# Layer 0's attention: row scores on 128 rows and two per column tile, output transposes two heads later

## The chip, the core and the metric

The kernel runs on one core of one Trainium2 chip. The metric is the device time of one execution in microseconds, as the median of several runs. Inside the core five engines work side by side and wait for each other through semaphores: TensorE (PE, matmuls and transposes into PSUM), VectorE (DVE), ScalarE (ACT), GpSimd (POOL) and SyncE (SP, which issues the DMAs). A matmul on TensorE has a weight load of its own (PEld), which may run beside an earlier matmul.

## What is computed

The whole kernel is two layers of attention and feed-forward work on x of 2 x 1024 x 128. The change touches the attention of layer 0 alone: 16 heads of width 8, causal, on 2 batches.

```python
def _L0_attn_ref(x, Wq, bq, Wk, bk, Wv, bv, Wo, bo):      # batch 2, seq 1024, 16 heads of 8
    q = x @ Wq.T + bq
    k = x @ Wk.T + bk
    v = x @ Wv.T + bv
    q, k, v = (split(q), split(k), split(v))
    scores = jnp.einsum('bhqd,bhkd->bhqk', q, k) / jnp.sqrt(jnp.float32(HEAD_DIM))
    scores = jnp.where(mask, scores, jnp.float32(NEG))     # causal
    attn = jax.nn.softmax(scores, axis=-1)
    out = jnp.einsum('bhqk,bhkd->bhqd', attn, v)
    out = out.transpose(0, 2, 1, 3).reshape(batch, seq, D_MODEL)
    return out @ Wo.T + bo

x = x + _L0_attn_ref(xn, ...) + _L0_ffn_ref(xn, ...)
```

## The kernel before

The program is a row of stages, each with its own block: projections of layer 0, attention of layer 0 (`attend_layer0`), experts, projections of layer 1, trees, attention of layer 1, and the end. Attention of layer 0 goes over 32 heads (2 batches x 16), one head after the other. Each engine has its own program, written out by hand as a `section(n, ...)` for each head n; four sections stand ahead of a loop, the loop holds four (`heads`), and five stand behind it (the last, n = 32, only finishes). Nothing but the order of the code and the semaphores sets what runs when.

Each score is computed twice. First the **row scores** (`row_unit`, L350, with the causal mask added by a second matmul, L353): the queries lie on partitions, 12 units of 128 to 512 keys per head, into two PSUM banks `ps_row` that are used in turn. VectorE reads each unit for its maximum (`peaks`, L463), so a unit can be written only when the unit two before it has been read (`row_read`). From the maxima VectorE makes a shift in three bfloat16 parts (L466 to L472, `shift_ready`). TensorE turns the shift into a row (L394, eight small matmuls of 3 weight columns), and ScalarE copies it into three spare rows of q, partitions 64 to 66 (L439); k holds ones there. So the second computation, the **column scores** (L407 and mask L410, 128 rows of contraction, keys on partitions, 8 tiles of 1024 down to 128 queries, two PSUM buffers `ps_col` in turn), comes out with the row maximum taken off. ScalarE takes the exponent of each tile (L445). The row scores use partitions 0 to 63 of q and k only, so the shift rows of an older head in the same q slot don't disturb them. q and k have four slots; SyncE loads the q and k of a head four ahead.

The **value products** of head n-1 (`pv`, L374, 32 output columns each, three groups) stand behind column tiles 0, 2 and 4 of head n. ScalarE copies their result from PSUM (L451, `oT`) between the exponents of tiles 5 and 6. TensorE turns `oT` by eight transposes of float32 (L424) into the same two `ps_row` banks, and VectorE adds up the four parts, divides and stores (`keep`, L481 to L487).

In section n of TensorE the order is: turn of head n's shift, two row units of head n+1, then each column tile of head n followed by one row unit of head n+1 (two behind tiles 0 and 2) and by a value product where one is due, then the transposes of head n-1 at the end. VectorE reads the 12 units of head n+1, makes its shift, then keeps head n-1. `row_base` counts the uses of `ps_row` for all of them.

## Time and profile before

| | |
|---|---|
| time, median of 3 runs | 2847.52 us (2844.19 to 2849.03) |
| profiled execution, its own time | 2842.8 us |
| its span, first to last instruction | 2840.7 us |
| attention of layer 0, first row unit to last store | 80.9 to 535.9 us |
| a steady head, query copy to query copy | 13.53 us |
| busy in 300 to 350 us: TensorE, VectorE, ScalarE, GpSimd | 46.30, 29.75, 25.14, 0.76 us |
| granted TensorE clock from 300 to 350 us | 1.00 of full |

The page cuts the span into 40 slices. Layer 0's attention lies in slices 2 to 8; TensorE is busy nine tenths or more in most of them, and PEclk is the share of full clock that it was granted:

```profile
PE   6799999999889688837676667667666766676668
...
DVE  4555655311245567668878787878887787878870
ACT  2345445433224133255656465656555564656543
...
PEclk7699999999879789966565666666665656665658
```

### The profile page before, as it was taken

To read this page: it belongs to the slowest core of one execution; us is meant where nothing else is said; L and a number is where in the kernel's file an instruction comes from. 1 tells how busy PE (TensorE), PEld (TensorE's weight loads), DVE (VectorE), ACT (ScalarE), POOL (GpSimd) and SP (SyncE) were. 2 spreads that over 40 slices of the span, in tenths; PEclk is the share of its full clock that TensorE was granted. 3 is DMA by queue.
4 is the path that set the end of the run, shared out by engine and by line. 5 is a ranking of instruction groups with operands and counts; after the bars stand their busy time and mean duration, and the time that the engine had idled before them with its cause. 6 is when DMAs were issued, how large, how long until landed. Compare 5 with 4: busy or idle time off the path is not lost. (4 is left out here: it accounts for less than half of the span.)

```text
span 2840.7 us, 38498 instructions
## 1 busy us (share of the span) xinstructions
PE 2149.0 (76%) x10704; PEld 1409.8 (50%) x10704; DVE 1863.7 (66%) x4939; ACT 1351.1 (48%) x2755; POOL 912.2 (32%) x708
## 2 busy tenths in 40 slices
PE   6799999999889688837676667667666766676668
PEld 3233333477654355515555454545554554555458
DVE  4555655311245567668878787878887787878870
ACT  2345445433224133255656465656555564656543
POOL 0000000000014100026455555556554645455650
PEclk7699999999879789966565666666665656665658
DMA  5000000100002000000000000000000000000000
GB/s 169 20 15 14 17 14 11 31 1 0 37 30 86 34 0 0 9 22 16 9 15 8 16 8 13 11 8 15 8 15 8 15 8 15 8 16 8 1 1 23
DMA packets 34022, 53.59 MB, mean 19 GB/s; under 512 B 9269, under 2 KB 15287, under 8 KB 33848
## 3 DMA queue, kind: packets, MB, share of 16 engines
q1 hardware_dynamic: 33847, 51.90, 6.3%
q14 instruction: 142, 1.16, 0.1%
q8 instruction: 33, 0.54, 0.1%
HBM read 34.04 MB, written 17.83 MB: 18 GB/s over the span
## 5 line engine op out<-in xcount | busy, mean ns | idle before, releaser
L1313 ACT ACTIVATE a_trash<-a_sc,a_search 128x1024 bf16<-128x1024 f32 (+6 forms) x672 | 548.5, 818 | 494.6 <-DVE a_npeak L1563 338.1
L1202 PE MATMUL a_ps_o<-g_v,a_kT 128*128 (+1 forms) x2304 | 501.6, 378 | 240.1 <-ACT a_kT L1330 235.1
L1202 PEld LDWEIGHTS a_ps_o<-g_v,a_kT 128*128 128x128 f32 x2304 | 458.0, 289 | 316.4 <-ACT a_kT L1330 262.4
L1191 PE MATMUL a_ps_t<-g_ident,a_prob 128*128 128x128 f32 x1152 | 286.2, 389 | 164.5 <-DVE a_prob L1547 164.5
L1179 PE MATMUL a_ps_s<-a_k,a_q 128*128 128x512 f32 (+3 forms) x768 | 359.9, 598 | 46.3 <-DVE a_sc L1557 34.1
L1261 POOL TENSOR_SCALAR a_work<-a_sc,a_thr 128x640 f32<-128x640 f32 (+3 forms) x128 | 213.1, 1669 | 505.8 <-POOLq L1291 505.8
L1244 POOL TENSOR_SCALAR a_prob<-a_sc,a_found 128x768 f32<-128x768 f32 (+4 forms) x160 | 282.9, 1768 | 223.1 <-POOLq L1242 223.1
L463 DVE TENSOR_REDUCE a_top<-a_ps_row 128x1 f32<-128x512 f32 (+3 forms) x384 | 207.5, 558 | 161.1 <-PE a_ps_row L353 107.2
L1191 PEld LDWEIGHTS a_ps_t<-g_ident,a_prob 128*128 128x128 f32 x1152 | 225.1, 230 | 174.5 <-issue 150.2
L1557 DVE TENSOR_SCALAR_CACHE_REDUCE a_sc<-a_ps_s 128x1024 f32<-128x1024 f32 (+7 forms) x256 | 193.3, 755 | 132.8 <-PE a_ps_s L1181 126.1
L1330 ACT ACTIVATE a_kT<-a_ps_t 128x512 f32<-128x512 f32 (+3 forms) x384 | 179.7, 476 | 204.7 <-PE a_ps_t L1191 204.6
L1179 PEld LDWEIGHTS a_ps_s<-a_k,a_q 128*128 128x128 f32 x768 | 151.5, 227 | 192.3 <-issue 114.6
L445 ACT ACTIVATE a_prob<-a_ps_col 128x1024 f32<-128x1024 f32 (+7 forms) x256 | 158.3, 653 | 148.5 <-PE a_ps_col L407 115.7
L1251 POOL TENSOR_TENSOR a_prob<-a_sc,a_prob 128x768 f32<-128x768 f32 (+4 forms) x160 | 201.9, 1270 | 0.0
L1323 ACT ACTIVATE a_prob<-a_sc,a_npeak 128x1024 f32<-128x1024 f32 (+7 forms) x256 | 180.6, 771 | 5.2 <-DVE a_sorted L1475 5.2
L938 POOL TENSOR_TENSOR p_full<-p_ra,p_rb 128x512 f32<-128x512 f32 x40 | 50.5, 1264 | 374.8 <-DVE p_rb L888 371.6
L331 POOL COPY a_v<-l_v 128x72 f32 (+1 forms) x32 | 8.0, 251 | 506.8 <-PE a_ps_out L374 428.7
L1547 DVE SCALAR_TENSOR_TENSOR a_prob<-a_sc,a_thr,a_prob 128x1024 f32<-128x1024 f32 (+2 forms) x96 | 124.5, 1326 | 65.2 <-issue 65.1
L1268 POOL TENSOR_TENSOR a_prob<-a_prob,a_work 128x640 f32<-128x640 f32 (+3 forms) x128 | 151.3, 1192 | 0.0
L584 ACT ACTIVATE ex_hid<-ex_ps_h,le_b 128x512 f32<-128x512 f32 x128 | 87.5, 687 | 128.1 <-PE ex_ps_h L561 127.8
L350 PE MATMUL a_ps_row<-a_k,a_q 64*128 64x512 bf16 (+3 forms) x384 | 132.4, 346 | 13.5 <-DMA a_k<-stack 12.5
L635 DVE SCALAR_TENSOR_TENSOR l_acc<-ex_ps_y,l_comb,l_acc 128x128 f32 x112 | 31.9, 345 | 151.4 <-PE ex_ps_y L552 151.1
(247 smaller groups left out, 3780.6 us busy)
## 6 DMA issues: line engine op xcount, KB each, us to landing
q1turned<-p_full SPq DMA_DIRECT2D x32, 256.0 KB, 2.0
a_q<-q1turned SPq DMA_DIRECT2D x32, 256.0 KB, 3.6
a_k<-k1turned SPq DMA_DIRECT2D x32, 256.0 KB, 4.0
stack<-p_parts SPq DMA_DIRECT2D x24, 256.0 KB, 3.8
a_q<-stack SPq DMA_DIRECT2D x32, 96.0 KB, 2.1
a_k<-stack SPq DMA_DIRECT2D x32, 96.0 KB, 2.2
le_w<-d_w SPq DMA_DIRECT2D x1, 2048.0 KB, 8.7
k1turned<-p_full SPq DMA_DIRECT2D x8, 256.0 KB, 2.0
```

The lines of the kernel that those rows point to most:

```text
L445: act.activation(prob[:, p, PO[j]:PO[j] + S - j * P], ps_col[:, (p + j + 1) % 2, 0:S - j * P], ACT.Exp, scale=SCALE).then_inc(col_read, 1)
L463: m = dve.tensor_reduce(top[:, i, c:c + 1], ps_row[:, u % 2, 0:width], AX.X, ALU.max)
L1179: pe.matmul(ps_s[:, j % 2, c:c + w], q[:, p, i * P:width], k[:, p, c:c + w], start=True, stop=True)
L1191: m = pe.transpose(ps_t[:, x % 2, a * P:(a + 1) * P], columns(prob, p, i)[:, (c + a) * P:(c + a + 1) * P], g.ident[:, :])
L1202: m = pe.matmul(outs[i // 4][:, i % 4, :], kT[:, x % 2, a * P:(a + 1) * P], v[:, bass.ds((n // GRP) * (TB * VW1) + (c + a) * VW1, VW1)], s ...
L1244: pool.tensor_scalar(columns(prob, p, i), columns(sc, p, i), found[:, i - 1:i], None, ALU.is_gt).then_inc(marked, 1)
L1251: pool.tensor_tensor(columns(prob, p, i), columns(sc, p, i), columns(prob, p, i), ALU.subtract).then_inc(aside, 1)
L1261: pool.tensor_scalar(marks(j), columns(sc, p, i), thr[:, i - 1:i], None, ALU.is_ge).then_inc(cut_marked, 1)
L1313: act.activation(trash[:, (p * NTAL + u) % 2, 0:(i + 1) * P], columns(sc, p, i), ACT.Sign, scale=-1.0, bias=trials[:, p, c, i - 1:i], accu ...
L1323: act.activation(columns(prob, p, i), columns(sc, p, i), ACT.Exp, scale=1.0 / DOWN, bias=npeak[:, p, i:i + 1]).then_inc(p_ready, 1)
L1330: act.activation(kT[:, x % 2, 0:cnt * P], ps_t[:, x % 2, 0:cnt * P], ACT.Copy).then_inc(t_read, 1)
L1557: dve.tensor_scalar(columns(sc, p1, i), ps_s[:, j % 2, 0:(i + 1) * P], SCALE, None, ALU.mult, ALU.max, accum_out=peak[:, p1, i:i + 1]).the ...
```

## The change

- Row units use all 128 rows of q and k. For that, the three shift rows of a q slot have to be zero again before the next head's row units: a zero tile `none` is added, and GpSimd writes zeros (`none + none`) into partitions 64 to 66 of the slot once all column tiles of its head are done (`clear`, semaphore `cleared`); the first row unit of a head waits for it.
- Behind every column tile stand two row units, until the 12 are used up (behind tile 4); behind tiles 5, 6 and 7 stand none.
- The transposes and the keeping of a head stand two sections later, and inside: TensorE turns head n-2 in section n behind column tile 0 and row units 2 and 3, ahead of the value product (`turn`); VectorE keeps it between its readings of units 3 and 4. Units 4 to 11 count two uses of `ps_row` later. In sections 0 and 1 there is none; section 32 has two.

```diff
+        none = r.sb("none", [P, S], BF16)
...
+        FIRST = 4
...
         def row_base(n):
-            if is_at(n, 0):
-                return NU
+            if is_at(n, 0) or is_at(n, 1):
+                return (n + 1) * NU
             if is_at(n, NH):
                 return row_base(NH - 1) + 2
-            return n * (NU + 2) + (NU - 2)
+            return n * (NU + 2) + (NU - 4)
+
+        def turn_base(n):
+            rows = not (is_at(n, NH - 1) or is_at(n, NH))
+            return row_base(n) + (FIRST if rows else 0)
...
+                def clear(n, h):
+                    pool.wait_ge(v_ready, n + 2)
+                    pool.wait_ge(col_ready, n * CU + CU)
+                    pool.tensor_tensor(q[SHIFT0:SHIFT0 + NSH, h, :], none[SHIFT0:SHIFT0 + NSH, :],
+                                       none[SHIFT0:SHIFT0 + NSH, :], ALU.add).then_inc(cleared, 1)
+                    pool.wait_ge(cleared, n + 1)
...
+                    for h in range(NQ):
+                        clear(i * NQ + (h - 2), (h + 2) % NQ)
+                        values(i * NQ + h, h % 2)
...
                     if u == 0:
                         pe.wait_ge(qk_in[h], i4 * 32 + 32)
+                        wait(pe, cleared, i4 * NQ + (h - NQ + 1))
                     wait(pe, row_read, unit - 1)
-                    last = pe.matmul(ps_row[:, u % 2, 0:width], q[0:SHIFT0, h, i * P:(i + 1) * P],
-                                     k[0:SHIFT0, h, c * CH:c * CH + width], start=True, stop=True)
+                    last = pe.matmul(ps_row[:, u % 2, 0:width], q[:, h, i * P:(i + 1) * P],
+                                     k[:, h, c * CH:c * CH + width], start=True, stop=True)
...
+                def turn(n, base):
+                    pe.wait_ge(out_read, n + 1)
+                    for x in range(2):
+                        pe.wait_ge(row_read, base + (x - 1))
+                        for i in range(4):
+                            m = pe.transpose(ps_row[:, x, i * P:(i + 1) * P],
+                                             oT[:, (4 * x + i) * P:(4 * x + i + 1) * P], g.ident[:, :])
+                        m.then_inc(row_ready, 1)
...
-                        rows_ahead(2 if j in (0, 2) else 1)
+                        rows_ahead(2)
+                        if j == 0 and not (is_at(n, 0) or is_at(n, 1)):
+                            turn(n - 2, turn_base(n))
                         if j in (0, 2, 4) and not is_at(n, 0):
                             pv(n - 1, 1 - p, j // 2)
                     rows_ahead(NU)
-                    if not is_at(n, 0):
...
+                    if is_at(n, NH):
+                        turn(NH - 1, turn_base(NH) + 2)
...
-                                act.wait_ge(row_ready, row_base(n - 1) + (2 if is_at(n, NH) else NU + 2))
+                                act.wait_ge(row_ready, turn_base(n) + 2)
...
                     for u, (i, c) in enumerate(UNITS):
+                        if u == FIRST and between is not None:
+                            keep(between, base + FIRST)
+                            base = base + 2
...
+                    turned = None if is_at(n, 0) or is_at(n, 1) else n - 2
                     if rows:
-                        peaks(n + 1, 1 - h % 2, row_base(n))
-                    if not is_at(n, 0):
-                        keep(n - 1, row_base(n) + (NU if rows else 0))
+                        peaks(n + 1, 1 - h % 2, row_base(n), turned)
+                    else:
+                        keep(turned, turn_base(n))
+                    if is_at(n, NH):
+                        keep(NH - 1, turn_base(n) + 2)
```

Three places show what the change makes of the instruction streams. A row is the line, the operation, its output and inputs and the output's size (`x4`: four in a row; REGISTER_ALU and ISA rows prepare or test a count). In the changed kernel the row unit is L372 with mask L375, the transposes L408, the value product L396, the column tile L440 with mask L443, and the shift's turn L427.

TensorE behind column tile 0, before:

```order
L350 MATMUL a_ps_row<-a_k,a_q 128x384
L353 MATMUL a_ps_row<-g_maskq,g_identb 128x128
L69 REGISTER_ALU
L350 MATMUL a_ps_row<-a_k,a_q 128x512
L353 MATMUL a_ps_row<-g_maskq,g_identb 128x128
L374 MATMUL a_ps_out<-a_prob,a_v 32x512 x4
L407 MATMUL a_ps_col<-a_q,a_k 128x512
```

The same place in the changed kernel:

```order
L372 MATMUL a_ps_row<-a_k,a_q 128x384
L375 MATMUL a_ps_row<-g_maskq,g_identb 128x128
L69 REGISTER_ALU
L372 MATMUL a_ps_row<-a_k,a_q 128x512
L375 MATMUL a_ps_row<-g_maskq,g_identb 128x128
L406 REGISTER_ALU
L408 MATMUL a_ps_row<-g_ident,a_oT 128x128 x4
L406 REGISTER_ALU
L408 MATMUL a_ps_row<-g_ident,a_oT 128x128 x4
L396 MATMUL a_ps_out<-a_prob,a_v 32x512 x4
L440 MATMUL a_ps_col<-a_q,a_k 128x512
```

The eight transposes now stand between row unit 3 and the first value product.

TensorE at the end of a head, from column tile 7 to the turn of the next head's shift, before:

```order
L407 MATMUL a_ps_col<-a_q,a_k 128x128
L410 MATMUL a_ps_col<-g_maskk,g_identb 128x128
L69 REGISTER_ALU
L350 MATMUL a_ps_row<-a_k,a_q 128x512
L353 MATMUL a_ps_row<-g_maskq,g_identb 128x128
L422 REGISTER_ALU
L424 MATMUL a_ps_row<-g_ident,a_oT 128x128 x4
L422 REGISTER_ALU
L424 MATMUL a_ps_row<-g_ident,a_oT 128x128 x4
L69 ISA
L392 REGISTER_ALU
L394 MATMUL a_ps_col<-g_identb,a_shift 3x128 x8
```

And in the changed kernel, from column tile 5 on:

```order
L440 MATMUL a_ps_col<-a_q,a_k 128x384
L443 MATMUL a_ps_col<-g_maskk,g_identb 128x128
L69 REGISTER_ALU
L440 MATMUL a_ps_col<-a_q,a_k 128x256
L443 MATMUL a_ps_col<-g_maskk,g_identb 128x128
L69 REGISTER_ALU
L440 MATMUL a_ps_col<-a_q,a_k 128x128
L443 MATMUL a_ps_col<-g_maskk,g_identb 128x128
L69 ISA
L425 REGISTER_ALU
L427 MATMUL a_ps_col<-g_identb,a_shift 3x128 x8
```

The last three column tiles stand in a row, with no row unit and no transpose between them and the shift's turn.

VectorE, from the end of a head's shift to the next unit, before (L472 makes the last part of the shift, L481 to L487 keep a head):

```order
L472 TENSOR_TENSOR a_shift<-a_left,a_shift 128x8
L69 REGISTER_ALU
L479 REGISTER_ALU
L481 TENSOR_REDUCE a_osum<-a_ps_row 128x36
L479 REGISTER_ALU
L481 TENSOR_REDUCE a_osum<-a_ps_row 128x36
L484 RECIPROCAL a_rec<-a_osum 128x8
L487 ISA
L487 REGISTER_ALU
L487 TENSOR_TENSOR l_o<-a_osum,a_rec 128x8x8
L462 ISA
L463 TENSOR_REDUCE a_top<-a_ps_row 128x1
```

In the changed kernel the keeping (L511 to L517) stands between the readings of units 3 and 4 (L493):

```order
L493 TENSOR_REDUCE a_top<-a_ps_row 128x1
L509 REGISTER_ALU
L511 TENSOR_REDUCE a_osum<-a_ps_row 128x36
L509 REGISTER_ALU
L511 TENSOR_REDUCE a_osum<-a_ps_row 128x36
L514 RECIPROCAL a_rec<-a_osum 128x8
L517 ISA
L517 REGISTER_ALU
L517 TENSOR_TENSOR l_o<-a_osum,a_rec 128x8x8
L492 REGISTER_ALU
L493 TENSOR_REDUCE a_top<-a_ps_row 128x1
```

The keeping moved from behind the shift to the middle of the next head's readings.

## Rows read from the trace of the kernel before

**Rows 1.** Windows: start:end, length, busy us (instructions) by engine, PEclk, DMA.

```profile
81.00:114.60 33.60, 28.61 (x102) 9.15 (x101) 17.32 (x39) 10.45 (x13) 0.00 (x0) 0.50 0.09 16
...
300.00:350.00 50.00, 46.30 (x313) 18.11 (x313) 29.75 (x77) 25.14 (x36) 0.76 (x3) 1.00 0.04 12
380.90:384.30 3.40, 2.52 (x19) 1.29 (x18) 1.92 (x10) 1.45 (x2) 0.00 (x0) 1.00 0.05 17
384.30:387.70 3.40, 3.40 (x14) 0.60 (x13) 1.24 (x2) 0.58 (x1) 0.00 (x0) 0.50 0.00 0
```

**Rows 2.** Timeline of TensorE, one head. Start, us, engine, line, out<-in, count, idle before.

```profile
315.50 0.39 PE L407 MATMUL a_ps_col<-a_q,a_k 128*128 128x512 bf16 x1 [0.41 <-ACT a_q L439]
315.72 0.22 PE L410 MATMUL a_ps_col<-g_maskk,g_identb 128*128 128x128 bf16 x1
315.78 0.38 PE L407 MATMUL a_ps_col<-a_q,a_k 128*128 128x512 bf16 x1
316.09 0.33 PE L350 MATMUL a_ps_row<-a_k,a_q 64*128 64x384 bf16 x1
316.36 0.23 PE L353 MATMUL a_ps_row<-g_maskq,g_identb 128*128 128x128 bf16 x1
...
316.99 1.07 PE L374 MATMUL a_ps_out<-a_prob,a_v 128*32 128x512 f32 x8
317.99 0.39 PE L407 MATMUL a_ps_col<-a_q,a_k 128*128 128x512 bf16 x1
...
321.01 0.39 PE L407 MATMUL a_ps_col<-a_q,a_k 128*128 128x512 bf16 x1
...
323.38 0.34 PE L407 MATMUL a_ps_col<-a_q,a_k 128*128 128x384 bf16 x1
...
325.47 1.37 PE L424 MATMUL a_ps_row<-g_ident,a_oT 128*128 128x128 f32 x8
327.32 0.61 PE L394 MATMUL a_ps_col<-g_identb,a_shift 128*3 128x128 bf16 x8 [0.47 <-DVE a_shift L472]
```

**Rows 3.** Timeline of VectorE, the same head's last readings and its shift.

```profile
324.24 1.89 DVE L463 TENSOR_REDUCE a_top<-a_ps_row 128x1 f32<-128x384 f32 x3 [1.03 <-PE a_ps_row L353]
...
327.09 0.17 DVE L472 TENSOR_TENSOR a_shift<-a_left,a_shift 128x8 bf16<-128x8 f32 x1
```

**Rows 4.** Timeline of ScalarE, the same head.

```profile
314.43 1.01 ACT L439 ACTIVATE a_q<-a_ps_col 3x1024 bf16<-3x1024 f32 x1 [2.30 <-PE a_ps_col L394]
316.27 1.02 ACT L445 ACTIVATE a_prob<-a_ps_col 128x1024 f32<-128x1024 f32 x1 [0.83 <-PE a_ps_col L407]
...
323.81 0.49 ACT L445 ACTIVATE a_prob<-a_ps_col 128x384 f32<-128x384 f32 x1 [1.02 <-PE a_ps_col L410]
324.20 1.02 ACT L451 ACTIVATE a_oT<-a_ps_out 128x1024 f32<-128x1024 f32 x1
325.10 0.56 ACT L445 ACTIVATE a_prob<-a_ps_col 128x256 f32<-128x256 f32 x2
327.96 1.01 ACT L439 ACTIVATE a_q<-a_ps_col 3x1024 bf16<-3x1024 f32 x1 [2.30 <-PE a_ps_col L394]
```

**Rows 5.** Timeline of TensorE's weight loads, around column tile 3.

```profile
321.02 0.10 PEld L410 LDWEIGHTS a_ps_col<-g_maskk,g_identb 128*128 128x128 bf16 x1
...
321.44 0.09 PEld L350 LDWEIGHTS a_ps_row<-a_k,a_q 64*128 64x128 bf16 x1
```

**Rows 6.** Groups of VectorE by line and shape, 150 to 500 us; count, busy us, mean ns.

```profile
L463 DVE TENSOR_REDUCE a_top<-a_ps_row 128x1 f32<-128x512 f32 x153 | 105.9, 692 | 39.7 <-PE a_ps_row L350 37.0
L463 DVE TENSOR_REDUCE a_top<-a_ps_row 128x1 f32<-128x384 f32 x51 | 28.5, 558 | 50.2 <-PE a_ps_row L353 50.2
```

**Rows 7.** The page's costliest groups: an elementwise step of GpSimd.

```profile
L938 POOL TENSOR_TENSOR p_full<-p_ra,p_rb 128x512 f32<-128x512 f32 x40 | 50.5, 1264 | 374.8 <-DVE p_rb L888 371.6
```

**Rows 8.** Timeline of ScalarE, two query copies in a row around 385 us.

```profile
382.10 1.01 ACT L439 ACTIVATE a_q<-a_ps_col 3x1024 bf16<-3x1024 f32 x1 [2.30 <-PE a_ps_col L394]
...
397.13 1.01 ACT L439 ACTIVATE a_q<-a_ps_col 3x1024 bf16<-3x1024 f32 x1 [2.30 <-PE a_ps_col L394]
```

More of the change, by code:

```diff
@@ L331, in values @@
                     pool.tensor_copy(v[:, p, :, 0:VW0], src.rearrange("p o (j w) -> p (o j) w", w=VW0)).then_inc(v_ready, 1)
-                pool.wait_ge(blank, 3)
+                def clear(n, h):
[4 more added lines that the diff above has]
+                    pool.wait_ge(cleared, n + 1)
+                pool.wait_ge(blank, 4)
                 values(0, 0, True)
                 values(1, 1, True)
-                with pool.Fori(1, NH // 2) as i:
-                    values(i * 2, 0)
-                    values(i * 2 + 1, 1)
+                clear(0, 0)
+                values(2, 0)
+                clear(1, 1)
+                values(3, 1)
+                with pool.Fori(1, NH // NQ) as i:
+                    for h in range(NQ):
+                        clear(i * NQ + (h - 2), (h + 2) % NQ)
+                        values(i * NQ + h, h % 2)
             @block.tensor
@@ L387, in rows_ahead @@
                             nh = (h + 1) % NQ
-                            row_unit(n + 1, i4 + (h + 1) // NQ, nh, row_base(n) + u, u)
+                            late = 2 if u >= FIRST and not (is_at(n, 0) or is_at(n, 1)) else 0
+                            row_unit(n + 1, i4 + (h + 1) // NQ, nh, row_base(n) + (u + late), u)
                     if not is_at(n, NH):
@@ L416, in section @@
                     rows_ahead(NU)
-                    if not is_at(n, 0):
-                        pe.wait_ge(out_read, n)
-                        base = row_base(n) + (NU if rows else 0)
-                        for x in range(2):
-                            pe.wait_ge(row_read, base + (x - 1))
-                            for i in range(4):
-                                m = pe.transpose(ps_row[:, x, i * P:(i + 1) * P],
-                                                 oT[:, (4 * x + i) * P:(4 * x + i + 1) * P], g.ident[:, :])
-                            m.then_inc(row_ready, 1)
+                    if is_at(n, NH):
+                        turn(NH - 1, turn_base(NH) + 2)
                 pe.wait_ge(blank, 4)
```

6 lines of the change are left out of this document (4 added, 2 removed).

## Prediction, made before the changed kernel ran

> **What bounds the kernel now.** I read the windows first, for the stage and its clock [rows 1], and then one steady head of layer 0's attention in the timelines of the three engines [rows 2 to 4]. The head is 13.53 us long (query copy to query copy, 314.43 to 327.96), and 29 heads of the 32 are like it. In [rows 2] the reader is to see that TensorE never stops between 315.50 and 325.47: it is the limit for those 10 us. Then comes a tail in which nothing but one chain counts: VectorE reads the last row scores, works out the shift and ends at 327.26 [rows 3], TensorE turns the shift (327.32), ScalarE copies it into q (327.96, 1.01 us) and only then can the next column tile start [rows 2, 4]. The eight output transposes (325.47, 1.37 us) stand inside that tail, beside VectorE's work, and cost nothing.
>
> **What goes: the switches.** In [rows 2] a matmul of 512 columns holds the engine 0.22 us (315.50 to 315.72) and the 128-column mask behind it 0.06 us. But 315.78 to 316.09 is 0.31, not 0.22, and 316.09 to 316.36 is 0.27 for 384 columns, where 0.16 to 0.17 would be in proportion. Both have a change between a 64-row and a 128-row matmul. [Rows 5] show why: the mask's weights load at 321.02 while the column matmul of 321.01 runs, but the 64-row load at 321.44 starts only when the matmul ahead has streamed. So each change costs 0.10 us. A head has 12 row units, 24 changes; three remain, since they border on 3- or 32-column weights. 21 x 0.10 = 2.1 us of TensorE's time per head goes. The Trainium skill ("TensorE: Matmul & The Clock Gate", Part 3, "The mechanism") says that a weight load overlaps a running matmul only where their row groups differ. By that, row units on all 128 rows would hide no load and the change would save nothing here. This trace disagrees: the 128-row loads at 321.02 are hidden behind a 128-row matmul.
>
> **What moves.** I walk a steady head of the changed kernel from its query copy = 0, with the trace's durations: 0.22, 0.16, 0.11, 0.06 us for 512, 384, 256, 128 columns, 0.10 for a change of weight shape, 0.05 from a reader's end to TensorE's start (315.44 to 315.50) and 0.27 from a final mask's start to its reader's. VectorE reads 512 columns in 0.69 and 384 in 0.56 [rows 6], back to back 0.08 less.
> - Column tile 0 at 1.06, streamed at 1.56, as before. Units 2 and 3 with masks: 2.05.
> - The transposes now stand here, in program order ahead of everything else. Their first bank is free once unit 2 is read: 1.72 + 0.27 + 0.56 + 0.05 = 2.59. The second waits for unit 3: 3.20. Four hold TensorE about 0.5 us (they give their result after 0.66: 326.18 to 326.84, [rows 2, 3]), so they end at 3.69. Value product: 0.10 + 1.00 (316.99 to 317.99) = 4.79. Before, this point was at 3.56 (317.99): **+1.23 us**. The transposes lose their cover.
> - Column tile 1, units 4 and 5, column tile 2: 5.93. Unit 6 wants unit 4 read: 5.22 + 0.38 + 0.04 + 0.69 + 0.05 = 6.39, a wait of 0.45. Units 6 and 7, second value product (0.99): 7.86. From 4.79 that is 3.07, before 3.02 (321.01): **+0.05**.
> - Column tile 3, units 8 and 9, column tile 4: 8.90. Unit 10 waits for unit 8's read until 9.35, unit 11 for unit 9's until 9.83. Third value product ends at 11.19. 3.33 us, before 2.37 (323.38), since two more units stand here and are waited for: **+0.96**.
> - The tail. The shift is ready at 12.25, early: VectorE's chain is now covered, 1 us to spare. What is late next is ScalarE. Its exponent of tile 5 cannot start before that tile, 11.61, and behind it in ScalarE's order stand the output copy (11.99, 1.02 us) and the exponent of tile 6 (12.90 to 13.29). The shift's turn writes the buffer that this last one reads. So 13.34 + 0.44 of turning + 0.22: the next query copy at 14.00. From the third product 2.81 us, before 4.58: **-1.77**.
>
> Sum: 1.23 + 0.05 + 0.96 - 1.77 = +0.47, 14.00 us for 13.53. The wait for tile 6's exponent is TensorE's sequencer's now, ahead of eight loads; the trace does not show that wait as the last one. Nearest is ScalarE's start 0.12 us after the column tile at 316.16, where the sequencer waits (0.04 elsewhere), so 0 to 0.1 us; I take 0.05: 14.05, **+0.52 x 29 = +15.1 us**. Bounds for all small terms together are 0.15 us a head either way, 10.6 to 19.5.
>
> The rest: heads 0 and 1 have no transposes inside and keep their switches' gain, at half clock [rows 1], and row scores of head 0 gain too: -2 to -5 us, I take -3. At the end the transposes of head 30 no longer run beside head 31's products: +1. GpSimd's clearing of three q rows is one elementwise step; 1.26 us for 512 columns [rows 7], so 1.3 to 2.5 us here. It waits for a head's last column tile and is wanted three heads later; its engine is busy 0.76 of 50 us otherwise [rows 1]. Queued behind it is the values' copy, wanted in the next head. Cost 0. The added zeroing of a tile at the start is covered by the wait for the first q and k.
>
> **The clock.** The granted clock is at half its full 2.4 GHz at the stage's start and full later [rows 1], except in three short stretches. Just before the one of 384.30 TensorE was busy for 2.52 of 3.40 us, around a shift's tail, and in it the clock was 0.50 for 3.4 us. It costs 1.5 us: the head of 382.10 lasts 15.03 [rows 8]. In the new head TensorE waits five times for VectorE (0.54, 0.12, 0.45, 0.45, 0.25) and then from 11.57 to 15.06 runs little but one column tile, the shift and two small units, some 1.3 us of work in 3.5. That is less than in any stretch of before. So more drops are likely; I take four more at 1.3: +5 us. The Trainium skill (same page, "A second HAM failure mode: psum-queue depth-cycling") tells of a kernel whose small stops between groups while cycling through PSUM buffers made the clock swing between its two levels. That speaks against this change, and is the second rival.
>
> Total: 15.1 - 3 + 1 + 5 = +18. The profiled execution took 2842.8 us (span 2840.7), the median 2847.5; I add the difference to the median: **2865 us**.
>
> **Rivals.**
> - *VectorE keeps up (faster).* The point that decides is whether a bank has been read when TensorE asks for it. If so, the five waits (1.81 us) vanish, the head takes 12.2 us, -1.35 x 29 = -39, and the time is about 2808. For it: VectorE is busy only 29.75 of 50 us [rows 1]. Against: two units in a row hold TensorE 0.4 us, reading two takes 1.3, and there are two banks. Chance 0.10.
> - *The clock drops in every second head or more.* 15 drops x 1.5 = 22 over the walk's +13: 2883; in nearly every head, 2904. Chance 0.20.
> - *The switches stay*, because the load waits for something other than the row count, or by the rule of the page. Walked again with 0.10 us at each change, and with much of it under waits that are there anyway, the head takes 14.62 us, 0.62 more than above; x 29 and the early heads' 3 us are +21: 2886. Against it stand the loads of [rows 5]. Chance 0.05.
> - *The walk is right in kind but long*, the early heads gain 5 and no clock drops are added: +5 to +9, 2853 to 2857; at 0.15 us a head less than that it is within 0.2%. Chance 0.15.
>
> The forecast itself, 2858 to 2872, has 0.50. The range takes in the short walk and the more moderate clock case: 2850 to 2888. A measurement of this kernel can tell about 0.2% (5.7 us). Faster 0.10, within 0.2% 0.07, slower 0.83.
>
> **What will show it.** Period of the query copies 14.0 to 14.1 us. TensorE's column and row matmuls 0.22 apart at 512 columns with no 0.10 between, and the weight loads of row units ahead of the matmuls. First transpose 1.5 us after column tile 0 starts, waiting for VectorE's reading of the rows. VectorE's shift done about 1 us before the shift is turned, and the turn waiting for ScalarE's exponent of tile 6 (256 columns) behind the output copy. Drops of the clock: count in the windows. If the turn of the shift still waits for VectorE, the walk's tail is wrong; if the period is under 13.3, the row waits are; if over 14.8, the switches or the clock are.

## The result, and the profile after

The changed kernel takes **2859.73 us** (median of 5 runs, 2855.05 to 2865.69). The kernel before, run beside it, takes 2846.91 us (5 runs, 2843.41 to 2849.03). The ratio is 1.0044, with a 95% interval of 1.0032 to 1.0056: slower by 0.44%. Forecast were 2865 us in a range of 2850 to 2888, slower.

The profiled execution of the changed kernel, the fastest of its five, took 2855.05 us, with a span of 2853.1 us, 12.4 us more than the span of before. Layer 0's attention, from its first row unit to its last store, lies from 80.4 to 546.6 us: 466.2 us, where before it was 455.0. What stands behind it takes 2306.5 us (before 2304.8). So 11.2 of the 12.4 us are in the stage that the change touches.

The page's tenths of TensorE and its clock, in 40 slices (the stage is slices 2 to 8):

```profile
PE   6677777899888788846676666667666766667668
...
PEclk6899999999969889976666666656565656665658
```

TensorE is less busy there than before, 7 tenths in several slices where nine and more stood. The windows say the same in numbers (start:end, length, busy us and instructions of PE, PEld, DVE, ACT, POOL, then the clock and DMA):

```profile
81.00:96.40 15.40, 11.62 (x48) 4.67 (x47) 9.85 (x23) 4.42 (x5) 0.00 (x0) 0.50 0.10 14
...
300.00:350.00 50.00, 38.32 (x286) 17.12 (x286) 27.13 (x73) 24.13 (x36) 8.29 (x7) 0.97 0.06 16
```

The second row answers to that of [rows 1]: TensorE 38.32 us busy in 50 instead of 46.30, VectorE 27.13 instead of 29.75, GpSimd 8.29 instead of 0.76 (it clears now). No engine is full, and the head got longer: waits set it. The first row shows half clock at the stage's start up to 96.40; before, it lasted to 114.60.

One steady head of TensorE, with the places that the walk names (start, us, engine, line, operation, out<-in, count, idle before it and who ended that). The query copy that begins it (ScalarE's copy of the turned shift into q, L466) is at 288.21, so subtract that from each time:

```profile
289.28 0.39 PE L440 MATMUL a_ps_col<-a_q,a_k 128*128 128x512 bf16 x1 [0.72 <-ACT a_q L466]
...
289.56 0.38 PE L440 MATMUL a_ps_col<-a_q,a_k 128*128 128x512 bf16 x1
289.78 0.33 PE L372 MATMUL a_ps_row<-a_k,a_q 128*128 128x384 bf16 x1
289.94 0.22 PE L375 MATMUL a_ps_row<-g_maskq,g_identb 128*128 128x128 bf16 x1
...
290.81 1.25 PE L408 MATMUL a_ps_row<-g_ident,a_oT 128*128 128x128 f32 x8 [0.38 <-DVE a_top L493]
291.99 1.06 PE L396 MATMUL a_ps_out<-a_prob,a_v 128*32 128x512 f32 x8
...
294.60 0.50 PE L372 MATMUL a_ps_row<-a_k,a_q 128*128 128x512 bf16 x2 [0.29 <-DVE a_top L493]
...
297.57 0.86 PE L372 MATMUL a_ps_row<-a_k,a_q 128*128 128x512 bf16 x2 [0.29 <-DVE a_top L493]
...
300.37 0.23 PE L440 MATMUL a_ps_col<-a_q,a_k 128*128 128x128 bf16 x1 [0.42 <-ACT a_prob L472]
...
301.63 0.61 PE L427 MATMUL a_ps_col<-g_identb,a_shift 128*3 128x128 bf16 x8 [0.98 <-ACT a_prob L472]
```

The 0.10 us at a change of rows is gone: 289.56 to 289.78 is 0.22 and 289.78 to 289.94 is 0.16, where [rows 2] had 0.31 and 0.27. In their place stand waits for VectorE's readings (290.81, 294.60, 297.57). And the shift's turn at 301.63 waits for ScalarE, not for VectorE's shift as before [rows 2]. ScalarE in the same head shows why:

```profile
288.21 1.01 ACT L466 ACTIVATE a_q<-a_ps_col 3x1024 bf16<-3x1024 f32 x1 [0.60 <-PE a_ps_col L427]
...
299.82 0.49 ACT L472 ACTIVATE a_prob<-a_ps_col 128x384 f32<-128x384 f32 x1 [1.91 <-PE a_ps_col L443]
300.21 1.02 ACT L478 ACTIVATE a_oT<-a_ps_out 128x1024 f32<-128x1024 f32 x1
301.11 0.56 ACT L472 ACTIVATE a_prob<-a_ps_col 128x256 f32<-128x256 f32 x2
302.28 1.01 ACT L466 ACTIVATE a_q<-a_ps_col 3x1024 bf16<-3x1024 f32 x1 [0.60 <-PE a_ps_col L427]
```

The output copy (300.21, 1.02 us) stands between the exponents of tiles 5 and 6, and the one of tile 6 begins at 301.11. VectorE had the shift ready at 300.43, 1.2 us ahead of its turn:

```profile
300.26 0.17 DVE L502 TENSOR_TENSOR a_shift<-a_left,a_shift 128x8 bf16<-128x8 f32 x1
```

The head is 302.28 - 288.21 = 14.07 us, against 13.53 before.

### The profile page after: what moved, and what is told of

It reads as the page before. It is cut to its first block and busy times, and to the rows that moved or that the text cites. A ratio compares the mean times of both kernels' runs of the same rounds, so it can differ in the third digit from the quotient of the medians.

```text
span 2853.1 us, 38627 instructions
## 1 busy us (share of the span) xinstructions
PE 2096.9 (73%) x10704; PEld 1406.1 (49%) x10704; DVE 1861.2 (65%) x4940; ACT 1352.8 (47%) x2755; POOL 968.9 (34%) x738
## 5 line engine op out<-in xcount | busy, mean ns | idle before, releaser
L493 DVE TENSOR_REDUCE a_top<-a_ps_row 128x1 f32<-128x512 f32 (+3 forms) x384 | 196.9, 553 | 157.9 <-PE a_ps_row L375 103.5
L472 ACT ACTIVATE a_prob<-a_ps_col 128x1024 f32<-128x1024 f32 (+7 forms) x256 | 159.8, 653 | 210.0 <-PE a_ps_col L440 150.7
L440 PE MATMUL a_ps_col<-a_q,a_k 128*128 128x512 bf16 (+3 forms) x384 | 111.4, 335 | 36.9 <-ACT a_q L466 23.5
L372 PE MATMUL a_ps_row<-a_k,a_q 128*128 128x512 bf16 (+3 forms) x384 | 109.8, 344 | 34.6 <-DVE a_top L493 19.3
```

Of the source, the lines that this page charges most:

```text
L472: act.activation(prob[:, p, PO[j]:PO[j] + S - j * P], ps_col[:, (p + j + 1) % 2, 0:S - j * P], ACT.Exp, scale=SCALE).then_inc(col_read, 1)
L493: m = dve.tensor_reduce(top[:, i, c:c + 1], ps_row[:, u % 2, 0:width], AX.X, ALU.max)
```

## The experiments

**Theory A** is the prediction's walk: the rows on 128 partitions save time, and the order takes more than that back, in three places: the transposes ahead of the value product, row units in pairs on two banks, and ScalarE's output copy ahead of the exponent for which the shift's turn waits. **Rival B**: GpSimd's clearing, the one new piece of work, costs the time. **Rival C**: the clock, which falls to half for short stretches, costs it. Each experiment is a kernel of its own, timed beside the kernel before on the same chip. "Head" is the steady distance of two query copies in its trace, "stage" is from first row unit to last store. All compute what the reference asks; `e9` does so with another rounding. What stands behind the stage is the same code in all of them, and yet it takes between 2301.6 and 2309.9 us in the profiled executions (before: 2304.8; e9, told below, is outside). So a few us in the total are not the edit's; the head and the stage are the measure.

### The 128 rows alone

`e1_rows128` is the kernel before with the wide rows, the zero tile and the clearing. The order stays.

```diff
+                def clear(n, h):
+                    pool.wait_ge(v_ready, n + 2)
+                    pool.wait_ge(col_ready, n * CU + CU)
+                    pool.tensor_tensor(q[SHIFT0:SHIFT0 + NSH, h, :], none[SHIFT0:SHIFT0 + NSH, :],
+                                       none[SHIFT0:SHIFT0 + NSH, :], ALU.add).then_inc(cleared, 1)
...
-                    last = pe.matmul(ps_row[:, u % 2, 0:width], q[0:SHIFT0, h, i * P:(i + 1) * P],
-                                     k[0:SHIFT0, h, c * CH:c * CH + width], start=True, stop=True)
+                    last = pe.matmul(ps_row[:, u % 2, 0:width], q[:, h, i * P:(i + 1) * P],
+                                     k[:, h, c * CH:c * CH + width], start=True, stop=True)
```

> The kernel before with one part of the change alone: row units on 128 rows, and GpSimd's clearing of the shift rows for it. Theory A (the walk: each change between a 64-row and a 128-row matmul exposes a weight load of 0.10 us, 21 of them a head; the order of the work is what costs): the changes go from a stretch in which TensorE never waits, a steady head takes 12.4 us instead of 13.53, some -35 us in the heads and -3 to -5 in the first two, about 2808 us. Rival B (what slows the changed kernel is the 128 rows themselves or the clearing, or the clock, which drops more often since TensorE is done sooner and waits more): a head of 13.5 or more, 2845 to 2860 us.

Measured: 2840.19 us, ratio 0.9973 (0.9961 to 0.9985). Head 13.01 us, but 11 of the heads took about 14.6 and one 15.0; stage 446.8. That is faster than before, and lies between what theory A (2808 us) and rival B (2845 to 2860 us) gave. Two things were not foreseen. The first is in VectorE's shift (first row) beside GpSimd's clearing (second):

```profile
306.32 0.79 DVE L482 TENSOR_TENSOR a_peak<-a_top 128x8 f32<-128x8 f32 x1
...
305.20 1.89 POOL L339 TENSOR_TENSOR a_q<-a_none 3x1024 bf16<-3x1024 bf16 x1 [0.75 <-PE a_ps_col L426]
```

VectorE's step that takes the maximum over the two halves of `top` lasts 0.17 us elsewhere and 0.79 here. It ends at 307.11, just as the clearing ends (305.20 + 1.89 = 307.09). In before's order this step is in the chain that sets the tail, so a head pays the whole 0.62 us. The second is the clock, in windows around one of the long heads:

```profile
306.70:310.10 3.40, 1.58 (x18) 0.88 (x17) 2.38 (x11) 1.01 (x1) 0.39 (x1) 1.00 0.13 33
310.10:313.50 3.40, 3.40 (x16) 0.78 (x15) 1.45 (x3) 1.02 (x1) 0.00 (x0) 0.51 0.00 0
```

TensorE was busy 1.58 of 3.40 us, around the tail, and in the next 3.40 the clock is at 0.51 (1.2 GHz instead of 2.4). Eleven times 1.6 and once 2.0 us are some 20 us.

### The same, with the clearing later

`e6_rows128_clear_late` lets the clearing wait for three column tiles more, into the next head's beginning. Then it starts behind the shift.

```diff
-                    pool.wait_ge(col_ready, n * CU + CU)
+                    pool.wait_ge(col_ready, n * CU + CU + 3)
```

> Row units on 128 rows in the order of before, with the clearing started behind the next head's column tile 1, where VectorE reads PSUM, instead of behind the last tile. Theory A: peak is 0.17 us again and the head 12.4 us; each drop of the clock, if they stay as frequent (12 in a stage), costs 1.6: 12.4 x 29 and 19 us of drops, about 2822 us. Rival B: 13.0 us a head, 2840 us. If VectorE's readings of PSUM are slowed by the clearing too, three of them show it.

Measured: 2798.66 us, ratio 0.9833 (0.9817 to 0.9850). Head 12.40 us, stage 410.7. One drop of the clock was left (at 104.0), where several were expected. Groups of VectorE by line and shape, and the clearing (count, busy us, mean ns):

```profile
L482 DVE TENSOR_TENSOR a_peak<-a_top 128x8 f32<-128x8 f32 x28 | 4.7, 167 | 1.0
...
L479 DVE TENSOR_REDUCE a_top<-a_ps_row 128x1 f32<-128x512 f32 x168 | 114.0, 688 | 34.2 <-PE a_ps_row L366 32.4
...
306.79 1.89 POOL L339 TENSOR_TENSOR a_q<-a_none 3x1024 bf16<-3x1024 bf16 x1 [7.51 <-PE a_ps_col L423]
```

In e1 the same group reads:

```profile
L482 DVE TENSOR_TENSOR a_peak<-a_top 128x8 f32<-128x8 f32 x28 | 21.9, 783 | 1.0
```

783 against 167 ns is 0.616 us, and the head went from 13.01 to 12.40, 0.61. So the clearing delays VectorE's step while both run, and nothing else of its costs is seen: the readings from PSUM, beside which the clearing runs now, keep their 688 ns ([rows 6]: 692). And the wide rows are worth 13.53 - 12.40 = 1.13 us a head in the old order. The prediction's price of the switches frees 2.1 us of TensorE. The rest did not reach the head; new waits stand in its place. Two of them in e6:

```profile
307.71 0.39 PE L366 MATMUL a_ps_row<-a_k,a_q 128*128 128x512 bf16 x1 [0.29 <-DVE a_top L479]
...
316.42 0.39 PE L423 MATMUL a_ps_col<-a_q,a_k 128*128 128x512 bf16 x1 [0.72 <-ACT a_q L455]
```

A row unit now waits for its bank to be read, and the wait for the query copy is 0.72 instead of 0.41 us, as the two small units beside it are done sooner. The shift's turn still waits for VectorE for 0.48, as before for 0.47 [rows 2].

The Trainium skill ("SBUF — State Buffer", "SBUF: two separate sides") says that VectorE and GpSimd share a pair of ports as an exclusive lock: a VectorE operation with two inputs in SBUF waits for a GpSimd operation that reads SBUF until that one is through. The end at 307.11 against 307.09 agrees with it, and so does that the PSUM readings are not slowed.

### The clearing alone

`e5_clear_only` is the kernel before with the clearing (the first part of e1's diff), for which nothing waits; rows stay at 64.

> The kernel before (row units on 64 rows, its own order) plus GpSimd's clearing of the shift rows, which nothing waits for here. In the 128-row kernel without the new order a steady head took 13.01 us where the walk gives 12.42, and the one row that differs is VectorE's maximum of the two halves (peak, 128x8), 0.79 us instead of 0.17, while GpSimd's clearing ran (1.89 us). Theory A (the clearing keeps VectorE's small step in SBUF waiting): the same here, since it falls in the same tail: peak 0.8 us, a head of 14.0 to 14.2 us, +0.5 to +0.6 x 29 = +15 to +18 us, about 2863 us. Rival B (the 0.6 us comes from the 128 rows): a head of 13.53, 2846 us.

Measured: 2898.40 us, ratio 1.0168 (1.0137 to 1.0199). The direction was right, the size not. The undisturbed heads are 14.10 us, as expected (0.57 over before), and the step on VectorE again takes 732 ns:

```profile
L481 DVE TENSOR_TENSOR a_peak<-a_top 128x8 f32<-128x8 f32 x24 | 17.6, 732 | 0.8
```

But after the first heads the clock fell in 15 stretches of 6.8 to 13.7 us, and many heads last 16 us and more. So 0.57 us of wait more in each tail brought, with the clock, 50 us in all. The clearing where the change puts it is thus a bad neighbour in before's order.

### The changed kernel with the clearing later

`e10_after_clear_late` is the changed kernel with the one line of e6.

> The changed kernel with GpSimd's clearing behind the next head's column tile 1. Theory A (in the changed order VectorE's shift is done before the clearing starts, so it keeps nothing waiting): 14.07 us a head, 2860 us as the changed kernel. Rival B (the clearing costs there too): up to 0.6 us a head less, 2842 us.

Measured: 2857.16 us, ratio 1.0034 (1.0023 to 1.0046), against 1.0044 (1.0032 to 1.0056) of the changed kernel itself: the intervals overlap. Head 14.07, to the hundredth the same. In the changed order the clearing at its first place costs a head nothing:

```profile
300.74 1.89 POOL L345 TENSOR_TENSOR a_q<-a_none 3x1024 bf16<-3x1024 bf16 x1 [0.75 <-PE a_ps_col L443]
```

This is in the changed kernel: the clearing starts at 300.74, and the shift was ready at 300.43. VectorE's step takes 167 ns here. So rival B is out for the changed kernel; what it says holds in before's order.

### The transposes back at the end

`e4_turn_at_end` is the changed kernel with the eight transposes and the keeping where they were, one head later; two row units still stand behind every column tile.

```diff
                         rows_ahead(2)
-                        if j == 0 and not (is_at(n, 0) or is_at(n, 1)):
-                            turn(n - 2, turn_base(n))
...
                     rows_ahead(NU)
-                    if is_at(n, NH):
-                        turn(NH - 1, turn_base(NH) + 2)
+                    if not is_at(n, 0):
+                        pe.wait_ge(out_read, n)
+                        base = row_base(n) + (NU if rows else 0)
+                        for x in range(2):
+                            pe.wait_ge(row_read, base + (x - 1))
+                            for i in range(4):
+                                m = pe.transpose(ps_row[:, x, i * P:(i + 1) * P],
+                                                 oT[:, (4 * x + i) * P:(4 * x + i + 1) * P], g.ident[:, :])
+                            m.then_inc(row_ready, 1)
```

> 128 rows and two row units per column tile as in the changed kernel, but the transposes and the keeping stay where they were, at the end of the head after. Theory A: two banks and two units in a row still make TensorE wait for VectorE, but the transposes stand beside the end of ScalarE's tail again: a head of 13.15 us, 29 to 31 heads x -0.4 and -4 in the first ones, about 2831 us. Rival B (where the transposes stand makes no difference): as the changed kernel, 14.07 us a head, 2860 us.

Measured: 2825.82 us, ratio 0.9931 (0.9914 to 0.9947). Head 13.17 us, stage 435.7, and no drop of the clock after the first heads. TensorE in its tail:

```profile
315.33 1.09 PE L440 MATMUL a_ps_row<-g_ident,a_oT 128*128 128x128 f32 x8 [0.70 <-ACT a_oT L467]
316.35 0.61 PE L410 MATMUL a_ps_col<-g_identb,a_shift 128*3 128x128 bf16 x8
```

The transposes wait for ScalarE's output copy here, and the shift's turn follows them. Even so the head is 0.90 us shorter than the changed one. So the move of the transposes costs 0.90 us a head. The remaining 13.17 - 12.40 = 0.77 against e6 is the price of two row units behind every tile (in both, the step on VectorE takes 167 ns). Together they are the 1.67 us between the changed head and e6's. The amounts of the experiments that follow lie inside these 1.67 us or overlap with them, and are not to be added to them.

### The transposes behind the product

`e11_turn_behind_product` is the changed kernel with two pieces of one line each exchanged: the value product ahead of the transposes behind column tile 0.

```diff
-                        if j == 0 and not (is_at(n, 0) or is_at(n, 1)):
-                            turn(n - 2, turn_base(n))
                         if j in (0, 2, 4) and not is_at(n, 0):
                             pv(n - 1, 1 - p, j // 2)
+                        if j == 0 and not (is_at(n, 0) or is_at(n, 1)):
+                            turn(n - 2, turn_base(n))
```

> The changed kernel with the transposes behind the first value product instead of ahead of it. Theory A: units 2 and 3 are read while the product runs, so the two waits ahead of the transposes (0.66 us) go, but the units behind the next column tile then wait for the keeping; the walk gives a head of 13.8 to 13.9 us, -0.2 x 29 = -6 us against the changed kernel, about 2854 us. Rival B (the transposes' place doesn't matter, their 1.0 us of work does): 14.07, 2860 us.

Measured: 2850.00 us, ratio 1.0012 (1.0002 to 1.0021). Head 13.81 us, stage 458.7.

```profile
301.73 1.06 PE L396 MATMUL a_ps_out<-a_prob,a_v 128*32 128x512 f32 x8
302.73 1.09 PE L408 MATMUL a_ps_row<-g_ident,a_oT 128*128 128x128 f32 x8
...
305.71 0.50 PE L372 MATMUL a_ps_row<-a_k,a_q 128*128 128x512 bf16 x2 [0.75 <-DVE a_top L493]
```

The transposes don't wait any more; the product covers VectorE's two readings. But VectorE now takes the pieces later, and row unit 6 waits 0.75 us instead of 0.29. Of what the wait cost, 0.26 us a head comes back.

### The output copy one exponent later

`e3_copy_behind_tile6` is the changed kernel with ScalarE's output copy behind tile 6's exponent.

```diff
-                        if j == 5 and not is_at(n, 0):
+                        if j == 6 and not is_at(n, 0):
                             act.wait_ge(pv_done, n)
```

> The changed kernel with ScalarE's output copy behind the exponent of tile 6 instead of tile 5, nothing else. Theory A (the tail of the new head is ScalarE's: exponent 5, output copy, exponent 6, then the turn of the shift): the turn no longer waits for the 1.02 us copy, then either VectorE's shift or exponent 6 is last; a head of 13.4 to 13.5 instead of 14.07, about -18 us against the changed kernel, 2842 us. Rival B (the tail is set by TensorE or VectorE): no change, 2860 us.

Measured: 2835.65 us, ratio 0.9967 (0.9953 to 0.9982). Head 13.49 us, as expected, stage 448.8. ScalarE, and below it TensorE's turn of the shift:

```profile
305.54 0.76 ACT L472 ACTIVATE a_prob<-a_ps_col 128x384 f32<-128x384 f32 x2 [1.91 <-PE a_ps_col L443]
306.19 1.03 ACT L478 ACTIVATE a_oT<-a_ps_out 128x1024 f32<-128x1024 f32 x1
...
307.42 1.01 ACT L466 ACTIVATE a_q<-a_ps_col 3x1024 bf16<-3x1024 f32 x1
...
306.66 0.61 PE L427 MATMUL a_ps_col<-g_identb,a_shift 128*3 128x128 bf16 x8 [0.29 <-ACT a_prob L472]
```

The exponents of tiles 5 and 6 follow each other at once (the first row), the buffer comes free, and TensorE turns the shift while the copy runs (306.66, in a copy from 306.19 to 307.22). The query copy now comes right behind tile 7's exponent, which starts at 307.10. One copy in the wrong place cost 0.58 us a head; this edit alone turns the change from slower to faster than before (its stage takes 448.8 us, before's 455.0). The medians fell by 24 us, more than the 18 expected; the stage became 17.3 us shorter in the profiled executions, and 3.7 us lie behind it, which no edit accounts for.

### Half the reading

`e9_half_read` is the changed kernel in which VectorE reads only half of the columns of each row unit (at least 128). The maximum that is taken off is then that of a part of the row; the exponents' quotient stays the same in exact arithmetic, but not its rounding.

```diff
-                        m = dve.tensor_reduce(top[:, i, c:c + 1], ps_row[:, u % 2, 0:width], AX.X, ALU.max)
+                        m = dve.tensor_reduce(top[:, i, c:c + 1], ps_row[:, u % 2, 0:max(P, width // 2)], AX.X, ALU.max)
```

> The changed kernel, but VectorE reads only half of each row unit's columns (at least 128) for its maximum; the rest of the computation is as it was. Theory A (with two units in a row and two banks TensorE waits for VectorE's readings, 1.8 us a head): the walk with readings of 0.29, 0.34 and 0.42 us gives a head of 12.9 to 13.0 us instead of 14.07, -31 us against the changed kernel, about 2828 us, or less if the drops of the clock go. Rival B (the readings are hidden beside TensorE's work): 14.07, 2860 us.

Measured: head 12.97 us, as expected (12.9 to 13.0): half of VectorE's reading time is worth 1.1 us of the 14.07. The total is another matter: 2855.13 us, ratio 1.0033 (1.0018 to 1.0047). The stage is 445.9 us long; in it 12 heads have a clock drop and are together 17.7 us longer than the others. And what stands behind the stage takes 2326.7 us instead of 2306.5. Layer 1's search loop runs until its data say so, and in this kernel its flag is loaded seven times more (the first row is there in the changed kernel too, the second is not):

```profile
L1569 DVEq TENSOR_LOAD <-a_flag x32: 300/314/558, 1266.1 to 2770.4; - x32
L1572 DVEq TENSOR_LOAD <-a_flag x7: 299/301/317, 2188.0 to 2207.0; - x7
```

That these loads are the 20 us is likely but not taken apart. So the total is no measure of this edit; the head is.

### The new order with 64 rows

`e2_order64` is the changed kernel with the row units on 64 rows again, and no clearing.

```diff
-                    last = pe.matmul(ps_row[:, u % 2, 0:width], q[:, h, i * P:(i + 1) * P],
-                                     k[:, h, c * CH:c * CH + width], start=True, stop=True)
+                    last = pe.matmul(ps_row[:, u % 2, 0:width], q[0:SHIFT0, h, i * P:(i + 1) * P],
+                                     k[0:SHIFT0, h, c * CH:c * CH + width], start=True, stop=True)
```

> The changed kernel with row units on 64 rows again and no clearing: the order alone. Theory A: 0.10 us more at each change of rows, part of it under waits: a head of 14.6 to 14.7 us, +31 to +34 us against before and no gain in the first heads, with some more drops of the clock 2880 to 2890 us. Rival B (the rows make nothing better): as the changed kernel, 2860 us.

Measured: 2945.21 us, ratio 1.0349 (1.0332 to 1.0367). The head is 17.07 us, not 14.6 to 14.7. Windows of one head:

```profile
291.30:294.70 3.40, 2.00 (x18) 1.07 (x16) 1.00 (x5) 2.50 (x5) 0.25 (x1) 1.00 0.21 58
294.70:301.50 6.80, 6.39 (x25) 2.46 (x25) 2.71 (x7) 1.38 (x2) 0.00 (x0) 0.50 0.00 0
301.50:311.70 10.20, 8.35 (x60) 3.14 (x58) 5.54 (x14) 5.47 (x9) 0.25 (x1) 1.00 0.06 19
```

From 124.0 us on every head has such 6.8 us at half clock (3.4 in the last), 17.07 us apart, each right behind a stretch in which TensorE had work for 2.00 of 3.40 us: the one around the shift's turn. Why it is every head here, and only a few in the changed kernel, no run shows. The walk's 14.6 us for full clock were never seen, so this run doesn't give the price of the switches in the new order. It shows that without the wide rows the new order would have cost 99 us instead of 13.

### Filling the waits

`e12_rows128_fill` is e1 with matmuls that nobody reads: four ahead of the wait for the shift, three ahead of the wait for the query copy.

```diff
                         wait(pe, col_read, n * CU - 1)
+                        for _ in range(FILL0):
+                            pe.matmul(ps_col[:, p % 2, 0:CH], k[:, h, 0:P], k[:, h, 0:CH], start=True, stop=True)
                         pe.wait_ge(shift_ready, n + 1)
...
                             if j == 0:
+                                for _ in range(FILL1):
+                                    pe.matmul(ps_col[:, (p + 1) % 2, 0:CH], k[:, h, 0:P], k[:, h, 0:CH],
+                                              start=True, stop=True)
                                 pe.wait_ge(col_read, n * CU + 1)
```

> The first experiment (128 rows in the order of before, 13.01 us a steady head and twelve heads of 1.6 us more, each with the clock at half) with seven extra matmuls per head that compute nothing wanted: four of 0.22 us where TensorE waits 1.2 us for the shift, three where it waits 0.9 us for the query copy. Theory A (the drops follow from these two waits coming close together): the drops go, the steady head stays 13.0 us, 12 x 1.6 = 19 us less, about 2821 us. Rival B (the drops come from elsewhere, the period of the head for one): twelve or so drops as before, 2840 us or, if the fill delays the shift, more.

Measured: 2820.04 us, ratio 0.9908 (0.9891 to 0.9924), with a head of 13.02 us. Windows of most of the stage, of e1 and then of e12:

```profile
81.00:500.00 419.00, 343.05 (x2475) 146.69 (x2475) 263.60 (x640) 201.44 (x300) 63.84 (x59) 0.93 0.06 15
```

```profile
81.00:500.00 419.00, 388.34 (x2837) 168.32 (x2837) 271.20 (x664) 214.21 (x319) 64.10 (x60) 0.99 0.06 15
```

The head is as long as e1's, VectorE's step still takes 783 ns, and all twelve drops are gone: 20 us less for more work. So in this kernel the drops follow from TensorE's waits (rival C is right as a mechanism, here). Little work in the tail is not the whole condition, though: in e6 TensorE is busy for 2.18 of 3.40 us there (313.00 to 316.40) and from the third head on the clock never falls, while before it fell behind a tail with 2.52 of 3.40 us [rows 1]. What else decides stays open. Where no drops are left there is nothing to win: see `e8_spread_fill` below.

### A version that is faster than both

`e7_spread_clear_late` is e6 with the row units spread 2, 2, 2, 1, 1, 1, 1, 0 behind the tiles, and the transposes at the end as before. It takes the two pieces of the change that pay (the wide rows, and one unit less at the end) without those that cost. `e8_spread_fill` adds one and three filling matmuls in e12's places.

```diff
-                        rows_ahead(2 if j in (0, 2) else 1)
+                        rows_ahead((2, 2, 2, 1, 1, 1, 1, 0)[j])
```

> As the last, with two row units behind column tiles 0, 1 and 2, one behind 3 to 6 and none behind 7 (the transposes at the head's end). Theory A: 12.15 us a head by the walk, about -40 us against before and -5 in the first heads without drops of the clock: 2800 us; with 12 drops, 2820 us. Rival B (an even spread makes VectorE the limit in the middle): over 12.5 us a head.

> As the last, with four extra matmuls per head that compute nothing wanted (128 rows, 512 columns, into a column buffer that is overwritten next): one ahead of the turn of the shift, three while TensorE waits for the query copy. Theory A (the clock falls after stretches in which TensorE does little; the fill stands where it would wait): a head as long as in the last kernel, 12.15 us, with fewer drops or none, so 0 to 19 us less than the last. Rival B (the drops don't follow from what TensorE does there): as many drops as without, or a longer head by up to 4 x 0.22 = 0.9 us.

Measured: e7 takes 2792.89 us, ratio 0.9809 (0.9793 to 0.9826), 1.9% faster than the kernel before. Head 12.12 us, stage 401.9. From 300 to 350 us TensorE is busy 41.82 us at full clock:

```profile
309.67 1.01 ACT L455 ACTIVATE a_q<-a_ps_col 3x1024 bf16<-3x1024 f32 x1 [1.49 <-PE a_ps_col L410]
321.78 1.01 ACT L455 ACTIVATE a_q<-a_ps_col 3x1024 bf16<-3x1024 f32 x1 [1.49 <-PE a_ps_col L410]
...
300.00:350.00 50.00, 41.82 (x341) 19.38 (x340) 31.98 (x86) 27.32 (x42) 8.68 (x9) 1.00 0.05 16
```

e8 takes the same 2792.89 us (ratio 0.9808, 0.9792 to 0.9825). Its clock is full from 93.3 us to the stage's end and its second head is faster (12.11 for 13.53 us), but it pays 0.07 us in each head, 12.19. In the stage 0.9 us are left of that (401.0 for 401.9); behind it, where e8 has a clock drop at 482.4, its profiled execution takes 0.9 us more.

## Why the prediction held, point by point

**What bounded the kernel, and the switches.** The walk stood on TensorE's load rows [rows 5]. In the changed kernel the row unit's weights load while the matmul ahead runs, and the distances are 0.22 and 0.16 us:

```profile
296.36 0.22 PE L440 MATMUL a_ps_col<-a_q,a_k 128*128 128x128 bf16 x1
296.36 0.15 PEld L372 LDWEIGHTS a_ps_row<-a_k,a_q 128*128 128x128 bf16 x2
```

The rule of the Trainium skill that the prediction quoted does not hold here as it was put: loads are hidden between matmuls of the same 128 rows. The rival in which the switches stay is out.

**The walk.** With the query copy at 0, the forecast's times and the trace's:

| step | forecast | measured |
|---|---|---|
| transposes start | 2.59 | 2.60 |
| their second four | 3.20 | 3.19 |
| first value product ends | 4.79 | 4.78 |
| unit 6 starts | 6.39 | 6.39 |
| column tile 3 | 7.86 | 7.86 |
| units 10 and 11 | 9.35, 9.83 | 9.36, 9.83 |
| column tile 5 | 11.19 | 11.18 |
| shift ready | 12.25 | 12.22 |
| output copy | 11.99 | 12.00 |
| exponent of tile 6 | 12.90 | 12.90 |
| shift's turn | 13.39 | 13.42 |
| next query copy | 14.05 | 14.07 |

The wait that the trace of before didn't show (TensorE's sequencer on ScalarE ahead of the turn) was bounded at 0 to 0.1 us and taken at 0.05; the turn stands at 13.42 and the next copy at 14.07, where without any wait they would be at 13.34 and 14.00, so it was 0.07 to 0.08. All three places are confirmed by runs that undo or lighten one: e4 and e11 for the transposes, e3 for the copy, e9 (half the reading) and e4 against e6 for the paired row units.

**The sum.** The forecast was right in sign and in its mechanism, and the steady head was right to 0.02 us. The three smaller terms were of another size. They do not cancel: all three came out lower than forecast, by 6.9 us together.

| term | forecast | measured |
|---|---|---|
| 29 steady heads | +15.1 (bounds 10.6 to 19.5) | 0.52 a head, +15.1 |
| first row units, heads 0 and 1 | -3 (-2 to -5) | -5.6 |
| the end, behind the last query copy | +1 | -0.6 |
| clock drops in the heads | +5 | +2.3 |
| sum in the stage | +18 | +11.2 |

(The steady heads are compared without their clock drops; the mean of before's is 13.55 us over all 29.) The span's other 1.2 us lie outside the stage (1.7 more behind it, 0.5 less ahead of it). The medians differ by 12.8 us where the two profiled executions differ by 12.3, so the way from one to the other by the medians' difference held.

The *early part* was mis-sized, outside its bounds: heads 0 and 1 took 13.41 and 13.05 us for 15.32 and 16.37, and the first stretch 10.35 for 10.77. The forecast left the clock as it was there; it reached full speed at 96.4 us instead of 114.6. That goes with the wide rows: in all eleven kernels with row units on 128 rows full clock first comes between 91 and 98 us, in the three with 64 rows (before, e5, e2) between 114 and 118. Why, no run shows. In e10, where only the clearing differs, full clock came at about 95 and heads 0 and 1 took 10.94 and 13.13 us, so this part moves by 2 us and more from one such kernel to the next. The *end*: before has a clock drop at 520.8 there, which the changed kernel doesn't have, and the forecast did not count on losing it. At the 1.5 us of before's other drops (an estimate) this alone makes -0.5 of the +1. The *clock*: five heads of the changed kernel have a drop (15.12 to 15.17 us, so some 1.05 each, 5.3 in all), against two of before (1.5 each, 3.0). I had four more at 1.3; there were three more, and each is cheaper, which fits with part of the slow work now lying beside waits that are there anyway; no run takes that apart. Windows around one of them:

```profile
243.20:246.60 3.40, 1.70 (x18) 0.99 (x17) 0.62 (x2) 2.17 (x4) 1.89 (x1) 0.99 0.19 58
246.60:250.00 3.40, 3.28 (x17) 2.05 (x19) 1.76 (x4) 1.02 (x1) 0.00 (x0) 0.50 0.00 0
```

It is the place that the prediction named: the shift's tail, TensorE busy for half of the stretch. The second rule quoted, of small stops while cycling through PSUM buffers, is borne out in part. The clock does fall where TensorE makes short stops, and with fillings in them the drops vanish (e12). But those fillings stand in the waits for the shift and for the query copy; in the waits for a `ps_row` bank, which the rule would point at, no run put any.

**GpSimd's clearing** was bounded at 1.3 to 2.5 us and measured 1.89 us; its cost of 0 is confirmed (e10). But the reason was incomplete: the prediction looked at who waits for it, not at whom it slows. In the changed order it starts 0.3 us after the shift is done, so that the cost of 0 came out right by luck; in before's order it costs 0.6 us a head (e1, e6).

**The rivals.** VectorE did not keep up: the waits are there. The clock drops in every second head did not come, though they are close by: e9, a variant of the same order, has them in 12 heads, e1 in 12, and e2 in nearly all. The measured 2859.73 us is in the forecast's own range of 2858 to 2872.

## What to carry to other kernels

Freed time on an engine is worth something only where that engine is the limit: of 2.1 us per head freed on TensorE, 1.13 came out in the old order, and a new order gave back 1.67 (14.07 - 12.40). When work is moved out of a tail because "TensorE is busy there", first ask what covered it in the tail and what the moved work waits for at its new place; a walk through one steady head with the trace's durations, in the order of each engine's own program, gave this to 0.02 us. And after such a change look again at the order of the engine that was never the limit: one ScalarE copy, one place later, was worth 0.58 us of each head.

## What the runs showed of the hardware

- An elementwise step of GpSimd on 3 partitions x 1024 bfloat16 takes 1.89 us, and VectorE's 128 x 8 step with two inputs in SBUF takes 0.79 us instead of 0.17 while it runs; readings of PSUM beside it stay at 0.69 us (e1, e6).
- A few tenths more of waiting in each head can cost far more through the clock: e5 has 0.57 us more per head and is 50 us slower; in e2 6.8 of each 17.07 us are at 1.2 GHz. In e6, whose tail is 0.6 us shorter than e1's, one drop is left, at 104.0. But before, with TensorE busier, has two in its steady heads and e6 none.
- With row units on 128 rows the clock first reached full speed at 91 to 98 us, with 64 rows at 114 to 118 (fourteen kernels); why is not shown.
- Matmuls that nobody needs, put into the waits, made a kernel 20 us faster (e12 against e1: 2820.04 and 2840.19 us).
- A stretch of 3.4 us at half clock costs 1.05 us in the changed kernel, 1.5 in the kernel before and 1.6 in e1. What makes the difference no run takes apart.
